# Another order of allocation in on-chip memory for a cross-attention block in split fp32r

## The reference

```python
tgt1 = layer_norm(tgt, g1, be1)
q, k, v = (tgt1 @ W.T + b for W, b in ((Wq, bq), (Wk, bk), (Wv, bv)))
score = einsum('bshd,bthd->bhst', q, k) / sqrt(16) + (1 - mask) * -1e9
tgt = tgt + einsum('bhst,bthd->bshd', softmax(score), v) @ Wo.T + bo
tgt = tgt + (memory @ Wg.T + bg)
tgt1 = layer_norm(tgt, g2, be2)
out = tgt + relu(tgt1 @ W1.T + b1) @ W2.T + b2
```

## The kernel before, in words

| kind | loads | streams |
|---|---|---|
| q, k | `wq`, `wk` | `xT` |
| v | `xT` | `wv` |
| up | `w1` | `zT` |
| down | `hT` | `w2` |
| output | `attnT`, `memT` | `wo`, `wg` |
| scores | `q_stack` | `k_stack` |
| values | `v_pad` | `probs` |
| transposes | `scores`, `xhat`, `xhat2`, `sum_inv` | `ident` |

## Time and profile before

### The profile page before, as it was taken

The page is one execution under the profiler, slowest core; times in us unless marked ns, Lnnn a source line. Parts: engine busy times, 40 slices in busy tenths (PEclk is TensorE's granted clock), DMA queues, the critical chain, the costliest instruction groups (busy, mean ns, idle before and its releaser), DMA issues.

```text
span 1761.2 us, 53553 instructions
## 1 busy us (share of the span) xinstructions
PE 1723.3 (98%) x17780; PEld 1696.0 (96%) x17780; DVE 1323.8 (75%) x6935; ACT 1435.8 (82%) x5577; POOL 800.4 (45%) x782
## 2 busy tenths in 40 slices
PE   5899999999999999999999999999999999999997
PEld 5799999999999999999999999999999999999997
DVE  7677777777777777777777777787777777777772
ACT  4888888888888888888888888888888888888882
POOL 4244444444444444444454454444444444444444
PEclk8899999999999999999999999999999999999999
DMA  5333333333333333333333333332433433433320
GB/s 169 109 127 107 115 123 108 117 121 107 120 121 106 121 120 107 122 118 109 121 118 103 127 112 105 131 118 95 134 116 96 135 113 100 134 112 103 126 80 25
DMA packets 185796, 200.46 MB, mean 114 GB/s; under 512 B 18864, under 2 KB 135984, under 8 KB 185520
## 3 DMA queue, kind: packets, MB, share of 16 engines
q1 hardware_dynamic: 185520, 197.02, 34.0%
HBM read 62.73 MB, written 16.78 MB: 45 GB/s over the span
## 4 chain that ended last, share of the span: by engine, by line
PE 95%; ACT 2%; DVE 1%; issue 0%; SPq 0%; DMA 0%; ACTq 0%; DVEq 0%
PE ffn_ps L808 13%; PE ffn_ps L810 13%; PE ffn_ps L809 13%; PE turn_ps L874 12%; PE work_ps L808 9%; PE work_ps L810 8%; PE work_ps L809 8%; PE score_ps L860 7%; PE value_ps L897 7%; PE work_ps L825 3%; ACT scores L388 1%; PE turn_ps L882 0%; ACT probs L400 0%; DVE xhat L556 0%; ACT hid L430 0%
## 5 line engine op out<-in xcount | busy, mean ns | idle before, releaser
L388 ACT ACTIVATE scores<-scores,row_min 128x128 f32<-128x128 f32 x2048 | 795.1, 402 | 2.3 <-DVE row_min L624 2.2
L738 POOL TENSOR_TENSOR hT_lo<-hid,hT_hi 128x512 fp32r<-128x512 f32 x256 | 355.0, 1387 | 511.9 <-DVE hT_hi L651 511.9
L624 DVE CUSTOM_DVE_ANT_0 scores<-score_ps,mask_bias 128x128 f32<-128x128 f32 x2048 | 472.4, 286 | 3.3 <-issue 2.9
L400 ACT ACTIVATE probs<-turn_ps 128x512 f32<-128x512 f32 x512 | 304.1, 595 | 163.0 <-PE turn_ps L874 163.0
L388 ACT ACTIVATION_READ_ACCUMULATOR scores<-scores,row_min 128x1 f32 x2048 | 411.1, 201 | 0.0
L874 PE MATMUL turn_ps<-ident,scores 128*128 128x128 f32 x2048 | 308.2, 273 | 5.3 <-ACT probs L400 5.2
L808 PE MATMUL ffn_ps<-zT_hi,w_lo 128*128 128x256 f32 x1024 | 302.2, 295 | 5.2 <-ACT hid L430 4.0
L808 PE MATMUL ffn_ps<-w_hi,hT_lo 128*128 128x256 f32 x1024 | 300.7, 294 | 2.4 <-ACT hid L430 2.4
L809 PE MATMUL ffn_ps<-zT_lo,w_hi 128*128 128x256 f32 x1024 | 285.5, 279 | 0.0
L810 PE MATMUL ffn_ps<-zT_hi,w_hi 128*128 128x256 f32 x1024 | 285.0, 278 | 0.0
L810 PE MATMUL ffn_ps<-w_hi,hT_hi 128*128 128x256 f32 x1024 | 284.7, 278 | 0.0
(11 more groups left out here) (112 smaller groups left out, 4187.1 us busy)
## 6 DMA issues: line engine op xcount, KB each, us to landing
q_stack<-q_hi SPq DMA_DIRECT2D x128, 256.0 KB, 2.4
k_stack<-k_hi SPq DMA_DIRECT2D x256, 128.0 KB, 2.3
x_in<-x_dram SPq DMA_DIRECT2D x64, 256.0 KB, 2.7
mem_in<-memory_dram SPq DMA_DIRECT2D x64, 256.0 KB, 3.3
x_res<-x_dram SPq DMA_DIRECT2D x64, 256.0 KB, 3.2
q_stack<-q_lo SPq DMA_DIRECT2D x64, 256.0 KB, 2.3
k_stack<-k_lo SPq DMA_DIRECT2D x128, 128.0 KB, 2.3
inv<-inv_cols SPq DMA_DIRECT2D x256, 64.0 KB, 2.1
```

The lines of the kernel that those rows point to most:

```text
L388: last = act.activation(exps, exps, ACT.Exp, bias=row_min[:, k, h:h + 1], scale=-1.0, accum_out=row_sum[:, k, h:h + 1])
L400: act.activation(probs[:, k, :], turn_ps[k % 2][:, :], ACT.Copy).then_inc(probs_copied, 1)
L624: last = dve.tensor_tensor_reduce(out=scores[:, slot(i, t), h, :], in0=score_ps[t % 2][:, h * S:(h + 1) * S], in1=mask_bias[:, b, :], scal ...
L738: pool.tensor_tensor(halves[1], src, halves[0], ALU.subtract).then_inc(done, 1)
```

## The change

The tiles are allocated in another order, and one tile of 32 bytes per partition (`spare`) is added that nothing uses. No instruction is added, removed or moved; only addresses differ.

```diff
+        xT = [...]; attnT = [...]; memT = [...]; hT = [...]     (each _hi and _lo)
+        row_min = sb("row_min", [P, CHUNKS, CH])
         weight("q", KT * D)
+        weight("g", KT * D)
+        one = sb("one", [P, H])
         weight("k", KT * D)
-        row_min, row_sum = sb("row_min", [P, CHUNKS, CH]), sb("row_sum", [P, CHUNKS, CH])
-        one = sb("one", [P, H])
+        weight("o", KT * D)
+        stats1 = sb("stats1", [P, GB, 6])
+        mv1 = sb("mv1", [P, GB, 2])
+        weight("v", KT * D)
+        row_sum = sb("row_sum", [P, CHUNKS, CH])
+        spare = sb("spare", [P, 8])
+        weight("2", FT * D)
         zT = [sb("zT_hi", [P, KT, ROWS], F32R), sb("zT_lo", [P, KT, ROWS], F32R)]
+        mv2 = sb("mv2", [P, GB, 2])
+        weight("1", KT * FF)
+        q_stack = [...]
+        var1 = sb("var1", [P, GB])
         k_stack = [...]
-        stats1 = sb("stats1", [P, GB, 6])
-        q_stack = [...]
-        for n in "vog":
-            weight(n, KT * D)
-        weight("1", KT * FF)
-        weight("2", FT * D)
+        var2 = sb("var2", [P, GB])
...
+        scores = ...; xhat = ...; xhat2 = ...; sum_inv = ...; probs = ...
+        stats2 = sb("stats2", [P, GB, 6])
+        carrier = sb("carrier", [P, CHUNKS])
         ident = sb("ident", [P, P])
+        v_pad = [...]
...
-        stats2 = sb("stats2", [P, GB, 6])
-        xT, attnT, memT, hT                                     (moved to the front)
```

More of the change, by code:

```diff
@@ L110, in weight @@
             weights[n] = (sb(f"w{n}_hi", [P, cols], F32R), sb(f"w{n}_lo", [P, cols], F32R))
+        xT = [sb("xT_hi", [P, KT, ROWS], F32R), sb("xT_lo", [P, KT, ROWS], F32R)]
+        attnT = [sb("attnT_hi", [P, KT, ROWS], F32R), sb("attnT_lo", [P, KT, ROWS], F32R)]
+        memT = [sb("memT_hi", [P, KT, ROWS], F32R), sb("memT_lo", [P, KT, ROWS], F32R)]
+        hT = [sb("hT_hi", [P, FT, ROWS], F32R), sb("hT_lo", [P, FT, ROWS], F32R)]
+        row_min = sb("row_min", [P, CHUNKS, CH])
         weight("q", KT * D)
+        weight("g", KT * D)
+        one = sb("one", [P, H])
         weight("k", KT * D)
-        row_min, row_sum = sb("row_min", [P, CHUNKS, CH]), sb("row_sum", [P, CHUNKS, CH])
-        one = sb("one", [P, H])
+        weight("o", KT * D)
[5 more added lines that the diff above has]
+        weight("2", FT * D)
         zT = [sb("zT_hi", [P, KT, ROWS], F32R), sb("zT_lo", [P, KT, ROWS], F32R)]
+        mv2 = sb("mv2", [P, GB, 2])
+        weight("1", KT * FF)
+        q_stack = [sb(f"q_stack{n}", [P, CPB, KT, ROWS], F32R) for n in range(2)]
+        var1 = sb("var1", [P, GB])
         k_stack = [sb(f"k_stack{n}", [P, CPB, 2, KT * GB, S], F32R) for n in range(2)]
-        stats1 = sb("stats1", [P, GB, 6])
-        q_stack = [sb(f"q_stack{n}", [P, CPB, KT, ROWS], F32R) for n in range(2)]
-        for n in "vog":
-            weight(n, KT * D)
-        weight("1", KT * FF)
-        weight("2", FT * D)
+        var2 = sb("var2", [P, GB])
         def tiles(n, k):
@@ L129, in xattn_block @@
         w1, w2 = tiles("1", KT), tiles("2", FT)
+        scores = sb("scores", [P, RING, CH, S])
+        xhat = sb("xhat", [P, GB, D])
+        xhat2 = sb("xhat2", [P, GB, D])
+        sum_inv = sb("sum_inv", [P, GB, KT, CPB, 2, COPIES])
+        probs = sb("probs", [P, CHUNKS, CH * S])
+        stats2 = sb("stats2", [P, GB, 6])
+        carrier = sb("carrier", [P, CHUNKS])
         ident = sb("ident", [P, P])
+        v_pad = [sb(f"v_pad{n}", [P, GB, H, 2 * HD]) for n in range(2)]
         row = sb("row", [P, 4, D])
@@ L135, in xattn_block @@
         x_in = sb("x_in", [P, GB, D])
-        xhat = sb("xhat", [P, GB, D])
         q = [sb("q_hi", [P, KT, ROWS], F32R), sb("q_lo", [P, KT, ROWS], F32R)]
         kk = [sb("k_hi", [P, KT, ROWS], F32R), sb("k_lo", [P, KT, ROWS], F32R)]
-        v_pad = [sb(f"v_pad{n}", [P, GB, H, 2 * HD]) for n in range(2)]
         mask_in, mask_bias = sb("mask_in", [P, GB, S]), sb("mask_bias", [P, GB, S])
-        scores = sb("scores", [P, RING, CH, S])
-        sum_inv = sb("sum_inv", [P, GB, KT, CPB, 2, COPIES])
         inv_cols = sb("inv_cols", [P, S])
-        probs = sb("probs", [P, CHUNKS, CH * S])
         inv = sb("inv", [P, KT, ROWS])
@@ L152, in xattn_block @@
         resid = sb("resid", [P, GB, D])
-        xhat2 = sb("xhat2", [P, GB, D])
         resid_b2 = sb("resid_b2", [P, GB, D])
@@ L172, in xattn_block @@
         bqc, bkc = qk_bias[:, 0:KT], qk_bias[:, KT:2 * KT]
-        mv1, mv2 = sb("mv1", [P, GB, 2]), sb("mv2", [P, GB, 2])
-        var1, var2 = sb("var1", [P, GB]), sb("var2", [P, GB])
-        carrier = sb("carrier", [P, CHUNKS])
         rstd1, rstd2 = sb("rstd1", [P, GB]), sb("rstd2", [P, GB])
```

## The result

The changed kernel takes 1776.38 us (median; 1774.57 to 1777.67) against 1762.8 us for the kernel before: 1.0075 times as long, 95% interval 1.0063 to 1.0088. It is slower by 13.6 us, where 1752 us was forecast.

The account below looks back on a forecast made before the run. PE's matmul spacing was taken as the bound; 0.169 (q, k, v) + 0.056 (up) - 0.056 (output) = 0.169 us per period, 10.6 us over 63 periods, gave 1752 us. Range for 8 in 10: 1729 to 1784.

Parts of the forecast that it names:

- The bound: Whole kernel: PE is busy 98% of the span, and the spacing of some 276 matmuls per period sets the time.
- Two paces, 4.7 ns apart: Product matmuls: fast 113.3 ns or slow 118, kept for a whole burst once entered, not caused by another engine.
- q, k, v: Their 36 matmuls per period, slow before, were taken to become fast: 0.169 us gained per period.
- Up: Up products, offset 448 to 480: slow third burst becomes fast, 0.056 us gained per period; 0.169 could be lost.
- Down: Down products, 48 matmuls with offset kept at 448: 0 change, with burst four (0.056 us) left open.
- Output: Output products wo and wg, 24 matmuls, nearly all fast: 0 to 0.113 us lost per period, half taken, 0.056.
- Scores, values, other engines: Three terms, each taken as 0; scores could move 0.075 us either way, values lose up to 0.075 per period.
- Transposes: 41 transposes per period, offset 0 to 96: taken as 0, with up to 0.193 us to lose.
- Rival 3: Transposes and values pay for leaving offset 0: 12 us cancels the gain, 1764 us; chance 0.08 on a partial gain.
- Rival 2: Away from 448 every product is slow, some a step worse, at q, k, v and output: 1780 us; chance 0.26.
- Rival 1: Address has no part in the two paces, so nothing happens: 1762.5 us; chance 0.17 with trades of equal gains and losses.
- Rival 4: A floor below 113.3 ns opens for some kinds of matmul: 1727 to 1738 us; chance 0.07.

Follow-up runs that it names:

- its first three variants: Changed kernel with up alone back at offset 448 (1765.45 us), with wg alone back at 448 (1775.58 us), and with both (1765.34 us).
- four other runs: k at 320 alone in the kernel before, 1762.3 us; all products at 320, 1782.83; k added to transposes at 96, 1769.08; changed kernel, transposes and values at 0, 1772.39.

## Why the prediction was wrong, point by point

- **The bound, right.** PE's spacing alone sets the time: +220 ns per period makes up the loss, with no new wait.
- **Two paces, 4.7 ns apart, not from another engine: right, and incomplete.** They are 113.3 and 117.8 ns, 4.5 apart. The earlier trace rows couldn't rule out another engine, since only the other products were absent there (from 1741.8 to 1752 us ACT was busy for 3.2 us and POOL for 5.1); the isolated matmuls do. Both are paces of offsets 64 and 192 modulo 256 alone. The other twelve of sixteen have paces of 116.3 to 120.4 ns and never reached 113.3. The kernel before was wholly at 448, one of the four good ones, so its trace could show only these two. This is where the forecast failed: it took the fast pace to be open at any offset.
- **q, k, v: 0.169 us taken as gained; 0.054 us was.** "Nothing shows it to be closed to q, k and v" was true of that trace and false of the kernel to come: 384 and 288 reached no fast pace, and both kinds stayed (+0.9 and +1.7 ns). k, at 320, could be fast and was (-56.6). k's gain hung on the rest of the layout: at 320 it was fast in the changed kernel and its first three variants and slow in four other runs, so that it came was luck. The term was mis-sized threefold for lack of a fact that a burst of isolated matmuls gives.
- **Up: 0.056 us taken as gained; 0.142 was lost.** "480 is only 32 bytes from 448" took nearness for likeness. The bound given for the loss, 0.169, held. This is the largest error, 0.198 of the 0.389 us per period between forecast and result, 12.5 us in all. That most of it belongs to up's own offset was shown by moving up alone (124 ns one way, 111 the other).
- **Down: taken as 0; 0.053 lost.** Burst four did turn fast, as was left open, but bursts two and three turned slow. The working priced an unchanged offset as unchanged time. Taking the transposes back in the changed kernel gave it back (-73 ns), and so did taking up back (-80 ns).
- **Output: 0.056 taken, 0.074 measured.** wg, at 128, paid 66 ns; wo, at 192, one of the good offsets, 8. The 0.056 was half of a bound, so that it came near is luck.
- **Scores, values, other engines: 0 taken, +11, 0 and nothing seen.**
- **Transposes: 0 for themselves, right** (-6 ns, and flat when isolated). Rival 3 is out. Their effect on bursts behind them was not in the sum: 60 ns lost here with the changed products, 100 won where all products are at 448.
- **Rival 2 gave the sign and nearly the time, 1780 to 1776.4, by a wrong place.** It had q, k and v paying; q and v stayed where they were and k won. Its deciding point, more of the 60 fast matmuls of up and output lose a step than of the 48 matmuls at the slow pace win one, is what happened: up's 36 and wg's 12 against k's 12. It was given 0.26 and the forecast 0.42. The one row of the trace on another offset, the single matmul at 286 ns, was no evidence for it: that offset is 64, which has the same two paces as 448 when isolated.
- **Rival 1 is out**: the order of allocation alone gave 1.0209 (all products at offset 0) and 1.0113 (320). **Rival 4** is out too: no product reached a lasting pace under 113.3.
- The Trainium skill, "TensorE: Matmul & The Clock Gate", section "Step-by-step: what each phase is for", says that loading the next stationary operand takes no read bandwidth from the running matmul. The runs don't agree that the two are independent: for fp32r at the upper clock the pace goes from 113.3 to 120.0 ns with the difference of their addresses.
- **What stays open.** Why the pace depends on the offset at all; what in the lead picks 113.3 or 117.8; and how the transposes' offset, which leaves their own pace alone, reaches the bursts behind them. Moving a kind also moves the offsets at its borders with other kinds. No run changed a border and left the kinds alone, so borders may be the way, and that isn't shown.

## What to carry to other kernels

For this shape (fp32r, load of 128 columns, stream of 256, back to back at the upper clock), allocate so that streamed minus loaded is 192 modulo 256 for every kind: when isolated it was fast behind 10 of 17 leads, 64 and 320 behind 4 and 5, and no other offset in its twelve tries. A layout with every operand aligned to 512 costs 2% here. For another shape measure anew: with a load of 64 columns, or a stream of 512, offset 0 has the lowest pace and 192 has one of the highest. Judge such an edit by the sum of all bursts of a period, not by the kind that was moved, and try the offset of the transposes as well, since it changes which bursts start fast and costs the transposes at most 6 of some 3740 ns per period. A trace in which one quantity has a single value can't price another value of it: measure the matmul alone first, one short run for all sixteen offsets.

## What the runs showed of the hardware that was not expected

- The pace of a load of 128 and a stream of 256 columns in fp32r at 2.4 GHz depends on (streamed - loaded) modulo 256 bytes: 120.0 ns at 0, 113.3 or 117.8 at 64 and 192, up to 120.4 at 96. At 1.2 GHz it didn't show between the two offsets that the runs have there. The first v burst runs at a granted clock of 0.50 in both kernels (24 to 26 us). Seven gaps take 25.67 - 24.18 = 1.49 us at offset 448 and 25.94 - 24.45 = 1.49 us at 288, 213 ns each; the first two rows are of the kernel before, the others of the changed one.

```profile
24.18 0.41 PE L809 MATMUL work_ps<-wv_lo,xT_hi 128*128 128x256 f32 x1
...
25.67 0.41 PE L810 MATMUL work_ps<-wv_hi,xT_hi 128*128 128x256 f32 x1
...
24.45 0.41 PE L813 MATMUL work_ps<-wv_lo,xT_hi 128*128 128x256 f32 x1
...
25.94 0.41 PE L814 MATMUL work_ps<-wv_hi,xT_hi 128*128 128x256 f32 x1
```

- The q burst of the earlier trace rows has the same 213 ns, but no row gives its clock: the profile's record of the clock begins at 17.0 us (16.8 in the changed kernel), and the view shows 1.00 for what lies ahead of it. That it ran at 1.2 GHz is inferred from the spacing, which falls to 113 to 118 ns about where the record begins.

- fp32 transposes of 128 columns kept 109.1 or 109.2 ns at all sixteen offsets, and their offset still changes the pace of products behind them.
- One program can take either of two times: ten runs of the kernel with transposes at 192 fell in two groups some 14 us apart (medians 1759.86 and 1773.88) at the same granted clock (0.991 to 0.994 in both). Only a run of the lower group was profiled, so where the others lose the time isn't shown; spread over 63 periods it would be 0.22 us each.
